# Delta-rule layer stack: triangular systems solved per two tiles in the 32x32 block layout, and the first stage of three of eight tiles placed inside the main loop

## What is computed

```
q, k, v = silu(causal_conv(x @ W))          # 4 taps, per channel
q, k    = l2norm(q), l2norm(k)
A       = strictly lower part of (beta * k) @ k.T     # 32 x 32
T       = (I + A)^-1                         # solved row by row
u, w    = T @ (beta * v), T @ (beta * k)
# then, chunk after chunk, with a state S (32 x 32 per head)
attn_i  = (q_i @ k_i.T) * causal
o_i     = q_i @ S + attn_i @ (u_i - w_i @ S);   S = S + k_i.T @ (u_i - w_i @ S)
```

## Time and profile before

| | us |
|---|---|
| runs | 999.03, 1008.98, 1000.93 |
| median | 1000.93 |
| the profiled execution, its own time | 1007.93 |
| its span, first to last instruction | 1006.0 |
| PE, PE weight loads, DVE busy | 843.8, 643.2, 640.0 |
| ACT, POOL busy | 494.2, 444.6 |
| start of the main loop (first matmul of the first `delta_wu`) | 230.6 |
| its share of the span before that point | 23% |

### The profile page before, as it was taken

One profiled execution on the slowest core, in us unless ns is written; L12 is line 12 of the kernel. 1 busy time (PEld: TensorE's weight loads), 2 busy tenths in 40 slices (PEclk: granted clock), 3 DMA queues, 4 the chain that ended last, 5 costly groups with the idle time before them and its releaser, 6 DMA issues.

```text
span 1006.0 us, 12279 instructions
## 1 busy us (share of the span) xinstructions
PE 843.8 (84%) x3874; PEld 643.2 (64%) x3874; DVE 640.0 (64%) x1190; ACT 494.2 (49%) x734; POOL 444.6 (44%) x339
## 2 busy tenths in 40 slices
PE   5999962027679679999999989999998999999986
PEld 3777751016448348678767857866886687676664
DVE  2554758994337457667668667766766677577452
ACT  3776723000234454564474466448446644866743
POOL 0534345992016306445435534543463454357343
PEclk9999965555559769999999999999999999999999
DMA  5234423001200200200120020011002000000000
GB/s 181 78 121 136 130 75 107 0 1 83 63 11 2 74 1 1 63 11 2 27 59 1 1 63 21 0 36 48 0 0 63 21 0 0 11 1 1 10 11 10
DMA packets 39973, 38.30 MB, mean 38 GB/s; under 512 B 1408, under 2 KB 34432, under 8 KB 39680
## 3 DMA queue, kind: packets, MB, share of 16 engines
q1 hardware_dynamic: 39936, 37.84, 12.9%
HBM read 23.16 MB, written 14.68 MB: 38 GB/s over the span
## 4 chain that ended last, share of the span: by engine, by line
PE 58%; DVE 11%; POOL 11%; ACT 10%; issue 8%; DMA 1%; ACTq 0%; SPq 0%; POOLq 0%; DVEq 0%
PE bank L319 57%; POOL opt L823 3%; POOL tmpg L820 3%; DVE m L1167 1%; DVE a L1102 1%; DVE sexp L1050 1%; ACT L756 1%; POOL acc L852 1%; DMA xt<-in_xh 1%; POOL fbl L844 1%; POOL fbl L865 1%; POOL wml L825 1%; POOL spread L802 1%; DVE yg L1060 1%; PE bank L382 1%
## 5 line engine op out<-in xcount | busy, mean ns | idle before, releaser
L844 POOL TENSOR_TENSOR fbl<-hf,fbh 128x512 fp32r<-128x512 f32 x64 | 83.1, 1298 | 134.7 <-DVE fbh L1073 134.7
L670 ACT ACTIVATE hf<-bank 128x512 f32<-128x512 f32 x64 | 38.3, 599 | 173.0 <-PE bank L319 171.7
L319 PEld LDWEIGHTS bank<-pk,spread 128*128 128x128 f32 x768 | 102.1, 213 | 26.1 <-issue 15.7
L319 PE MATMUL bank<-pk,spread 128*128 128x64 f32 x768 | 105.1, 298 | 14.3 <-issue 7.6
L865 POOL TENSOR_TENSOR fbl<-hf,fbh 128x512 fp32r<-128x512 f32 x32 | 44.1, 1379 | 105.8 <-DVE fbh L1129 105.8
L1071 DVE TENSOR_TENSOR fbl<-hf,fbh 128x512 fp32r<-128x512 f32 x64 | 61.8, 966 | 39.4 <-ACT fbh L672 39.4
L852 POOL TENSOR_TENSOR acc<-acc,yg 128x512 f32<-128x512 f32 x48 | 66.4, 1383 | 45.2 <-DVE yg L1060 45.2
L802 POOL TENSOR_TENSOR spread<-pk,cst 128x1024 f32<-128x1024 f32 x16 | 41.8, 2636 | 90.0 <-DVE pk L929 90.0
L319 PE MATMUL bank<-fal,wfh 128*128 128x512 f32 x160 | 65.8, 411 | 2.5 <-ACT hf L697 1.6
L861 POOL TENSOR_TENSOR fal<-hf,fah 128x512 fp32r<-128x512 f32 x32 | 41.6, 1300 | 53.4 <-DVE fah L1124 53.4
L1060 DVE TENSOR_TENSOR yg<-bank,gb 128x512 f32<-128x512 f32 x64 | 43.8, 684 | 32.2 <-PE bank L319 32.2
(11 more groups left out here) (216 smaller groups left out, 2326.1 us busy)
## 6 DMA issues: line engine op xcount, KB each, us to landing
pack<-pk SPq DMA_DIRECT2D x8, 1280.0 KB, 5.9
pk<-pack SPq DMA_DIRECT2D x8, 1280.0 KB, 7.1
xt<-in_xh SPq DMA_DIRECT2D x16, 262.0 KB, 3.0
ws<-in_wf SPq DMA_DIRECT2D x8, 352.0 KB, 3.2
stg<-in_wm SPq DMA_DIRECT2D x1, 2048.0 KB, 7.9
tt<-ttc SPq DMA_DIRECT2D x1, 2048.0 KB, 6.3
out<-f SPq DMA_DIRECT2D x8, 256.0 KB, 2.8
tb<-tt SPq DMA_DIRECT2D x7, 256.0 KB, 7.2
```

The lines of the kernel that those rows point to most:

```text
L319: return P.matmul(out, lhsT, rhs, start=start, stop=stop, skip_group_check=skip)
L670: A.activation(hf[:, 0, :], bank[4][:, :], ACT.Gelu).then_inc(S["gelu_done"], 1)
L844: G.tensor_tensor(fbl[:, s, :], hf[:, 1, :], f32(fbh[:, s, :]), ALU.subtract)\
```

## The change

1. The systems are no longer solved at once after the first stage, but for two tiles at a time. DVE turns beta*(k.k) of two tiles (32 chunks) with one block transpose (`solve_in`), so that partitions are (head, chunk) and each step works on one system per partition: (31 - j)(j + 1) elements in all. PE and ACT have no part in it. DVE takes columns 0 to 7 (KD = 8), POOL the columns from 8 on, in steps 8 to 30. `solve_out` turns the result back and multiplies by beta, and SP stores it (`store_tt`), tile 0's T is loaded again by `load_tb(0)`.
2. Only tiles 0 to 4 (LEAD = 5) pass the first stage ahead of the main loop. Tile 5 is in dense(None, 0, None), tile 6 in tails(None, None, 0, None), tile 7 in tails(None, 0, 1, None).
3. The solve of tiles 0 and 1 lies between the first-stage work of tiles 2 and 3, that of tiles 2 and 3 in tile 4 and dense(None, 0, None), that of tiles 4 and 5 in the two tails, and that of tiles 6 and 7 in the turns of dense(1, 2, None).
4. The weights come in 19 pieces of 512 columns through two buffers, the expert weights too. x of the first stage has a buffer of its own (`xs`). silu(v) goes from ACT straight into the pack. Norms have one table load instead of two. The softplus steps of the recurrence's parameter stand in tile 1.

The diff, cut to its core:

```diff
+PIECES = ((0, 1), (2, 3), (4, 5), (6, 7), (8, 9, 10), (11, 12, 13), (14, 15, 16), (17, 18))
+LEAD = 5
+KD = 8
...
-            dense(None, 0, None)
-            tails(None, None, 0, None)
+            dense(None, 0, None, LEAD)
+            tails(None, None, 0, None, LEAD + 1)
             dense(0, 1, None)
-            tails(None, 0, 1, None)
-            dense(1, 2, None)
+            tails(None, 0, 1, None, LEAD + 2)
+            dense(1, 2, None, None, True)
             tails(0, 1, 2, None)
...
@@ SP, ahead of the main loop
+            for t in range(LEAD - 1):
+                load_xs(t + 2)
+                store_pack(t)
+                for p in PIECES[t + 1]:
+                    load_piece(p)
+            sp.wait_ge(S["pk_stored"], 16 * (LEAD - 1))
+            sp.dma_start(pk[:, :, 1:, :], io["pack"][:, 0:CT, :, :]).then_inc(S["pk_loaded"], 16)
+            store_tt(0)
+            sp.wait_ge(S["tt_stored"], 16)
+            load_tb(0)
+            store_pack(LEAD - 1)
...
@@ PE, dense
                 for e in range(E):
+                    if s1 is not None:
+                        if e == 0:
+                            beta(s1)
+                        if e < 3:
+                            project(s1, e)
+                        if e == 3:
+                            squares(s1)
+                        if e in (5, 6):
+                            gram(s1, e - 5)
...
@@ ACT, tails
                 if A_:
                     act.wait_ge(*after("o_ready", a + 1))
                     A.activation(a2[:, :], a1[:, :], ACT.Square).then_inc(S["osq_done"], 1)
+                if s1 is not None:
+                    heads_in(s1, 0)
...
+                if s1 is not None:
+                    heads_in(s1, 1)
+                    heads_in(s1, 2)
+                    beta_in(s1)
...
+                if s1 is not None:
+                    norms(s1)
+                    high_parts(s1)
...
@@ POOL, ahead of the main loop and in dense
+            solve_init(0)
+            for t in range(LEAD):
+                key_spread(t, 0)
+                key_spread(t, 1)
+                low_parts(t)
+                if t >= 2:
+                    solve(t // 2 - 1, steps(t % 2))
+                if t == 3:
+                    solve_init(1)
...
+                    if s1 is not None and e in (0, 2):
+                        solve(s1 // 2 - 1, range(16, 23) if e == 0 else range(23, C - 1))
+                    if inv:
+                        solve(3, range(4 * e, min(4 * e + 4, C - 1)))
...
@@ DVE, ahead of the main loop
+            def solve_in(p):
+                dve.wait_ge(S["gram_read"], 4 * p + 4)
+                need(dve, "tt_stored", 16 * p)
+                V.transpose(apm[:, :, :], kkp[:, :, :].rearrange("p c j -> p j c")).then_inc(S["inv_in"], 1)
+            def solve(p, rows):
+                for j in rows:
+                    n, k, done = C - 1 - j, min(j + 1, KD), (C - 1) * p + j
...
+                    tt(m, a, r, ALU.mult).then_inc(S["tv_mul"], 1)
+                    dve.wait_ge(S["tv_mul"], done + 1)
+                    tt(o, o, m, ALU.subtract).then_inc(S["tv_step"], 1)
+            def solve_out(p):
+                dve.wait_ge(S["tv_step"], (C - 1) * (p + 1))
+                dve.wait_ge(S["tg_step"], (C - 1 - KD) * (p + 1))
+                V.transpose(ttp[:, :, :].rearrange("p c i -> p i c"), tpm[:, :, :]).then_inc(S["t_turned"], 1)
...
+            for t in range(LEAD):
+                if t >= 2 and t % 2:
+                    solve(t // 2 - 1, steps(t % 2)[:8])
+                unit_rows(t)
+                value_rows(t)
+                beta_rows(t)
+                if t >= 2 and t % 2 == 0:
+                    solve_in(t // 2 - 1)
+                    solve(t // 2 - 1, steps(t % 2)[:8])
...
+                centre_pieces(t)
+                if t >= 2:
+                    solve(t // 2 - 1, steps(t % 2)[8:])
+                if t == 3:
+                    solve_out(0)
+                if t + 2 <= LEAD:
+                    split_x(t + 2)
+                gram_rows(t, 0)
+                gram_rows(t, 1)
...
@@ DVE, dense
+                if inv:
+                    solve_in(3)
                 if a is not None:
                     delta_spread(a, 0)
                 for e in range(E):
+                    if s1 is not None:
+                        if e < 4:
+                            solve(s1 // 2 - 1, steps(1)[4 * e:4 * e + 4])
+                        if e == 4:
+                            solve_out(s1 // 2 - 1)
+                            unit_rows(s1)
+                            value_rows(s1)
+                            beta_rows(s1)
+                            centre_pieces(s1)
+                            split_x(s1 + 1)
+                        if e == 6:
+                            gram_rows(s1, 0)
+                    if inv:
+                        solve(3, range(4 * e, min(4 * e + 4, C - 1)))
...
+                if s1 is not None:
+                    gram_rows(s1, 1)
+                    solve_in(s1 // 2)
+                if inv:
+                    solve_out(3)
...
@@ DVE, tails
+                if s1 is not None:
+                    solve(2, steps(s1 % 2)[0:5])
                 if M_:
                     scale("2", m, m1, m3, x2).then_inc(S["x2"], 1)
...
+                if s1 is not None:
+                    value_rows(s1)
+                    beta_rows(s1)
+                    centre_pieces(s1)
+                    solve(2, steps(s1 % 2)[5:8])
                 if A_:
                     dve.wait_ge(*after("gelu_done", 3 * E * a))
                     scale("1", a, bank[3], a4, x1).then_inc(S["x1_hi"], 1)
...
                 hi1(2)
+                if s1 is not None:
+                    unit_rows(s1)
+                    if s1 + 1 < NT:
+                        split_x(s1 + 1)
...
                 hi2(1)
+                if s1 is not None:
+                    gram_rows(s1, 0)
...
                 hi2(3)
+                if s1 is not None:
+                    gram_rows(s1, 1)
+                    solve(2, steps(s1 % 2)[8:])
+                    if s1 == NT - 1:
+                        solve_out(2)
```

More of the change, by code:

```diff
@@ new lines, in dense, with tails @@
+            def dense(m, a, f, s1=None, inv=False):
+                if s1 is not None:
+                    load_xs(s1 + 1)
+                    store_tt(1)
+                    store_pack(s1)
+                    for p in PIECES[s1 + 1]:
+                        load_piece(p)
+                if inv:
+                    store_tt(3)
+                    sp.wait_ge(S["tt_stored"], 64)
+            def tails(f, m, a, l, s1=None):
+                if s1 is not None and s1 + 1 < NT:
+                    load_xs(s1 + 1)
@@ L362, in _ @@
             pe.wait_ge(S["w_in"], 32)
             pe.wait_ge(S["wtap_done"], 1)
-            def stage1(t, s):
-                squares(t, s)
-                if not isinstance(t, int) or t + 1 < NT:
-                    project(t + 1, 1 - s)
-                gram(t, s)
-            project(0, 0)
+            beta(0)
+            for m in range(3):
+                project(0, m)
             pe.wait_ge(S["cst_in"], 16)
@@ L522, in hidden, with tails @@
                         i.then_inc(S[done], 1)
-            def tails(f, m, a, l):
+            def tails(f, m, a, l, s1=None):
+                if s1 is not None:
+                    beta(s1)
+                    project(s1, 0)
                 if f is not None:
                     last = f + 2 if m is not None else NT
+                    if isinstance(f, int) and f == 0:
+                        pe.wait_ge(S["ws_lo"], NPIECE)
                     pe.wait_ge(*after("x3_ready", f + 1))
@@ L866, in tails @@
                             .then_inc(S["fb_ready"], 1)
+                if s1 is not None:
+                    solve(2, steps(s1 % 2))
+                    key_spread(s1, 0)
+                    key_spread(s1, 1)
+                    low_parts(s1)
+                    if s1 == NT - 1:
+                        solve_init(3)
                 if a is not None and (not isinstance(a, int) or a < NT - 1):
```

635 lines of the change are left out of this document (349 added, 286 removed).

## The result

The changed kernel is slower, by 1.4%. Its median is 1020.33 us (1015.73 to 1021.54, 4 runs) beside 1004.95 us for the kernel before on the same chip (999.03 to 1009.54, 4 runs): ratio 1.014, with a 95% interval of 1.010 to 1.018. The forecast was 981 with a range up to 1016, reckoned from the first three of these four runs (1000.93). The profiled execution took 1021.54 us with a span of 1019.7, so 13.7 more than the span of 1006.0 before.

What follows compares the result with a forecast made beforehand. PE was taken to bound the first stage and a serial DVE and POOL solve the 81 us after it. Terms -87 + 11 + 18 + 0 + 22 + 16 = -20 us gave a 981 us median, range 946 to 1016.

Steps and rivals of the forecast that it cites:

- Up to the main loop, -87: Everything ahead of the first `delta_wu`: it would start at 143.6 instead of 230.6, a gain of 87 us.
- dense(None, 0), 11: First dense, with tile 5 added: 11 us come back, bounds 0 (all hidden) to 19 (PE at half clock).
- half of both falls into waits: In dense(None, 0): half of PE's added 15 us and DVE's 18.3 falls into waits for the other, giving 11.
- tails(0), 18: Tails of tile 0 with tile 6 added: insertions into a serial chain give back 18 us; 10 at best, 27 at half clock.
- tails(1), 22: Tails of tile 1 with tile 7 added: the same insertions and more on DVE give back 22 us, bounds 12 and 28.
- dense(0, 1), 0: Dense between the two tails: its queues are unchanged, so nothing comes back.
- dense(1, 2), 16: Dense with the last pair's solve: DVE's steps ahead of lo0 hold PE up; 16 us come back, bounds 8 and 36.
- half clock: Rival, 20%: stalls in head and tails keep PE at half clock; losses of 90 us eat the gain, 1004 us.
- exclusive ports: Rival, 17%: DVE and POOL wait for each other's instructions in solves; +36 us, 1016 us; sign: 0.8 us steps in dense(1, 2).
- the first dense with an expert tile: Profile reading of the kernel before: PE is full in this window, busy 43.4 of 45 us.
- The 0.37 us of a DVE step: DVE step cost without waiting; the exclusive rival decides once it is 0.37 + 0.5, and steps near 0.37 would show hiding.
- 80 - 9 = some 8 us: Head: if POOL ran its steps at half the price, the first `delta_wu` would come some 8 us earlier.

Runs made afterwards that it cites:

- the order mended: Changed kernel with three SP reorderings: T's store ahead of pieces 8 to 10, pieces 13 and 16 behind other transfers; 1002.83 us, 0.998 of the kernel before.
- piece 16: Changed kernel with weight piece 16 loaded behind tile 7's x and tile 1's pack and T; 1018.1 us in one run.
- The best version: Changed kernel with three SP reorderings, all solve columns on DVE, and head order changed on SP, POOL and DVE; 994.40 us, 0.987 of the kernel before.

## Why the prediction was wrong

- **Up to the main loop, -87: right**, -84.9, by steps that erred both ways. POOL's steps 16 to 30 set the first `solve_out` as forecast, but took 14.1 us (96.6 to 110.7) and not 17. POOL's price of 4.9 ns per element came from the old solve, where its instructions waited for DVE's; it was 1.7 to 2 here. T's store behind the pieces and its load were in the working. DVE's `solve_in`, which waits for that store, was not: 3.8 us.
- **dense(None, 0), 11: the step that failed**, 28.9, beyond its upper bound of 19. Two things were missed in the queues. For the head I had put the store of T behind piece 10, but priced only what this does to the load of T, not to DVE's `solve_in`, which waits for the same store: 6.1 us in this stage. And the three pieces of the following groups were taken as loads that hide, without asking what is behind the third one while it waits for POOL: x of tile 6, 7.6 us. With the order mended the term is 15.4, where "half of both falls into waits" gave 11, and the 4.4 between stay open.
- **tails(0), 18 and tails(1), 22: right in kind**, 21.9 and 24.4, both within their bounds; piece 16 is 3 us of the first. The forecast's own list for tails(0) adds up to 19.6, or 16.7 without the 2.9 of `project(6, 2)`, not to 17 to 18.
- **dense(0, 1), 0: right**, 1.0.
- **dense(1, 2), 16: right in the main, mis-sized**, 24.1. PE waits for DVE, as forecast, though its long waits were for `spread` (9.6 us) and not for lo0 and lo1. Two things were not in the term. DVE's steps were priced without waiting: 0.165 us and 1.0 ns per element give 16.5 us for the 62, and they took 26.4. The price was right for an undisturbed step; the missing 9.8 us are waits for POOL's instructions, which the forecast had put into a rival only. And the half clock behind PE's pauses, which made about half of the steps' 20.2 us, was in no term. The transposes took 2 us each where 1.3 was reckoned.
- **The rivals.** The exclusive ports had 1016 us, nearest to what was measured. Their mechanism is in the rows, their price was not: DVE's steps lose 9.8 us in dense(1, 2) where the rival had 21, and 22 in the whole kernel, on the path or off it, where it had 36. A step took 0.43 us on average there, not the 0.8 that it named as its sign. Without POOL's steps dense(1, 2) is 5.5 us shorter, and with all columns on DVE the median is 7.9 us lower, head included; the order of the queue alone is worth 17.5. The half clock is real. In dense(1, 2) it follows from pauses and made about half of the steps' price. The time alone would have spoken for one cause, where there were three.
- **Slips.** The window called the first dense with an expert tile is that of dense(1, 2), the second. The 0.37 us of a DVE step in the rivals doesn't follow from the forecast's price, which gives 18.7 / 62 = 0.30. "80 - 9 = some 8 us" is no sum that comes out; nothing rests on it.

The best version is 1.3% faster than the kernel before. The order of the queue took the changed kernel from a loss of 1.4% to no change; all columns on DVE and the order at the head gave the rest.

What stays open: dense(1, 2) still costs 23 us. The steps there could be spread over more stages, but their buffers lie over those of the feed-forward, whose first write follows right behind, at 430.9 in the changed kernel; this wasn't tried. Why tails(0) fell by 3 us only with piece 16 moved was not taken apart further.

## What to carry to other kernels

When work moves into a loop, walk down every in-order queue once more and ask of each entry that can be held back (here a load that waits for a buffer): who waits for what is behind it. Give such an entry the last place among those that are ready. Price a pause of PE at more than its length: look at the granted clock of the microseconds behind it. And compare ends, not only durations, before calling two instructions side by side an overlap.

## What the runs showed of the hardware

- A block transpose of 1024 columns between a strided and a plain layout took 1.90 to 2.08 us (8 of them), where 512 columns took 0.70: nearly three times for twice the columns.
- A pause of PE of 3.4 us was followed by 6 us at a granted clock of 0.50, and after 3.0 us of pause by 5.7 us at 0.56; without the steps, and so without these pauses, the clock of the stage was 0.94.
- A DVE step that started over 0.165 us before the end of a running POOL instruction ended at the end of that instruction plus 1.0 ns per element (93 of 96, within 0.04 us). So 152 elements took 1.28 us instead of 0.31 behind 512 columns, and 136 elements 0.41 to 0.45 behind 108; only the fixed 0.165 us overlapped.
- POOL's small instructions, undisturbed, were cheaper than the rows of before had it: 23 elements 0.23 us, 135 elements 0.42 to 0.45, so 1.7 to 2 ns per element, where 2.55 and 4.9 had been worked out.
